# GpSimd's split of the value weights waits in addition for the scaled late values: an attention and mixture-of-experts block on one core

## The reference

```python
h = layernorm(x) * (1 + ca) + sa                      # x: 4 batches x 1024 tokens x 256
normed = h * rsqrt(mean(h * h) + EPS)
q, k, v = split(normed @ W_qkv.T + b_qkv)             # 16 heads of 64
scores = where(causal_mask, -inf, einsum('bqhd,bkhd->bhqk', q, k))
attn = softmax(scores, axis=-2)                       # over the QUERIES, for each key
x = x + ga * (einsum('bhqk,bkhd->bqhd', attn, v) @ W_o.T + b_o)
h = layernorm(x) * (1 + cb) + sb
x = x + gb * moe(h)                                   # 16 experts, top 1, 256 slots each
```

## Time and profile before

| what | value |
|---|---|
| median of 3 runs | 1401.01 us (1400.46 to 1401.9) |
| the profiled execution: its time, its span | 1402.89 us, 1401.1 us |
| busy: PE, PEld, DVE, ACT, POOL | 88%, 62%, 60%, 41%, 23% |
| mean granted TensorE clock | 0.941 of full speed; 0.89 from 60 to 351 us, 1.00 from 351 to 1036 us |
| attention steps with an odd `pp` | 16, with a split of the value weights at 92, 157, 222, 286, 351, 413, 475, 537, 599, 660, 722, 784, 846, 907, 968 and 1029 us |

### The profile page before, as it was taken

How to read it: one execution, slowest core, us unless ns; L and a number is a source line. 1 busy time by engine, 2 the same in 40 slices (tenths; PEclk the granted TensorE clock), 3 DMA queues, 4 the chain that set the end, 5 groups by cost and what they waited for, 6 DMA issues and landing times.

```text
span 1401.1 us, 24008 instructions
## 1 busy us (share of the span) xinstructions
PE 1235.5 (88%) x7256; PEld 867.0 (62%) x7256; DVE 839.9 (60%) x2166; ACT 574.4 (41%) x1387; POOL 325.7 (23%) x487
## 2 busy tenths in 40 slices
PE   2588888888999999999999999999988629999995
PEld 0455555555666666666666566666656518888884
DVE  4465656656766777677666666666665533444443
ACT  0354555555455555555555555455541001111110
POOL 2221111211232323222233312212221530111111
PEclk8788899999999999999999999999998859999998
DMA  5311111111222122221121121112155862565630
GB/s 194 127 65 58 65 57 64 57 45 43 69 65 71 64 66 83 67 68 64 63 71 64 64 80 60 55 58 74 60 188 201 290 216 101 176 239 180 227 109 18
DMA packets 99118, 139.55 MB, mean 100 GB/s; under 512 B 9848, under 2 KB 71162, under 8 KB 98808
## 3 DMA queue, kind: packets, MB, share of 16 engines
q1 hardware_dynamic: 90504, 113.81, 24.7%
q10 hardware_dynamic: 4464, 16.25, 2.8%
q0 software_dynamic: 4096, 8.82, 1.6%
HBM read 94.76 MB, written 48.00 MB: 102 GB/s over the span
## 4 chain that ended last, share of the span: by engine, by line
PE 77%; issue 8%; ACT 5%; DVE 4%; DMA 3%; SPq 2%; POOL 1%; DVEq 0%; ACTq 0%; POOLq 0%
PE SC L653 19%; PE Z L671 17%; PE Z L818 8%; PE SC L792 8%; PE XA L703 6%; PE XA L625 5%; ACT E L853 4%; PE XB L625 4%; PE XA L635 4%; PE XB L635 3%; PE XB L690 1%; DMA out<-th 1%; DMA xb<-xh_s 1%; DVE nm L1065 0%; SPq L443 0%
## 5 line engine op out<-in xcount | busy, mean ns | idle before, releaser
L853 ACT ACTIVATE E<-SC,nm 128x512 f32<-128x512 f32 (+7 forms) x512 | 375.5, 740 | 436.7 <-DVE nm L1065 436.7
L1065 DVE CUSTOM_DVE_ANT_0 SC<-SC,mask 128x512 f32<-128x512 f32 (+7 forms) x512 | 375.8, 786 | 226.4 <-PE SC L653 226.4
L653 PE MATMUL SC<-XQ,XK 64*128 64x512 f32 (+3 forms) x2304 | 271.3, 368 | 51.5 <-ACT E L853 50.1
L653 PEld LDWEIGHTS SC<-XQ,XK 64*128 64x128 f32 x2304 | 188.7, 192 | 151.2 <-issue 134.2
L671 PE MATMUL Z<-E,vs 128*64 128x512 f32 (+3 forms) x1536 | 271.8, 496 | 4.0 <-DVE vs L1043 4.0
L671 PEld LDWEIGHTS Z<-E,vs 128*64 128x64 f32 x1536 | 100.3, 138 | 141.8 <-issue 127.0
L818 PE MATMUL Z<-W,hh 128*128 128x256 f32 x512 | 114.9, 383 | 2.2 <-DVE yb L1311 2.2
L792 PE MATMUL SC<-bT,W 128*128 128x256 f32 x512 | 113.9, 381 | 0.0
L818 PEld LDWEIGHTS Z<-W,hh 128*128 128x128 f32 x512 | 97.3, 192 | 15.6 <-DVE yb L1311 2.6
L792 PEld LDWEIGHTS SC<-bT,W 128*128 128x128 f32 x512 | 98.0, 192 | 13.4
L853 ACT ACTIVATION_READ_ACCUMULATOR E<-SC,nm 128x1 f32 x512 | 101.3, 198 | 0.0
(11 more groups left out here) (193 smaller groups left out, 1753.7 us busy)
## 6 DMA issues: line engine op xcount, KB each, us to landing
W<-in_w SPq DMA_DIRECT2D x32, 1024.0 KB, 8.5
z_s<-zs ACTq DMA_DIRECT2D x31, 512.0 KB, 2.6
zt<-z_s SPq DMA_DIRECT2D x24, 512.0 KB, 3.7
W<-in_wqk SPq DMA_DIRECT2D x33, 257.0 KB, 2.7
slots_s<-zt SPq DMA_DIRECT2D x16, 520.0 KB, 4.0
xb<-slots_s SPq DMA_DIRECT2D x16, 520.0 KB, 3.7
xb<-xh_s SPq DMA_DIRECT2D x24, 256.0 KB, 5.4
Wv<-in_wv SPq DMA_DIRECT2D x17, 256.0 KB, 2.6
```

The source lines that it names most:

```text
L653: last = pe.matmul(SC[h][:, at:at + z - a], XK[rows, ap, kp, lo:lo + P], XQ[rows, ap, qp, a:z], start=(t == 0), stop=(t == 2))
L853: act.activation(E[:, h, EOFF[kb]:EOFF[kb + 1]], SC[h][:, at:at + S - lo], ACT.Exp, bias=nm[:, h, kb:kb + 1], scale=-1.0, accum_out=rs[:, ...
L1065: dve.tensor_tensor_reduce(SC[h][:, at:at + S - lo], SC[h][:, at:at + S - lo], mask[:, 0:S - lo], 1.0, BIG, ALU.add, ALU.min, nm[:, h, kb: ...
```

## The change

GpSimd waits, before it splits the value weights at the end of an odd step, in addition for the third (late) scaling of values of that step. The work itself stays as it is.

```diff
                         pool.wait_ge(auxa_full, st.of("auxa", piece_use(st, ("v", 2))[1]))
                         pool.wait_ge(auxb_full, st.of("auxb", piece_use(st, ("v", 3))[1]))
+
+                        pool.wait_ge(s["vscaled"], st.of("vscaled", LATE + 1))
                         split_values_weights(st.b * COUPLES + st.j + 2)
```

## The result

The changed kernel takes 1389.56 us in the median of 17 runs (1386.2 to 1392.84), beside 1401.69 us for the kernel before, also 17 runs (1391.65 to 1405.15). The ratio is 0.9924, 95% interval 0.9905 to 0.9943: 8 to 13.3 us faster, 10.7 in the middle. Forecast were 9.1 us, with a time of 1391.9 in a range of 1386 to 1396.5. The profiled execution has a span of 1389.7 us instead of 1401.1.

A forecast was written before the change was run, and what follows sets the result against it. TensorE carries 77% of the chain and waits where GpSimd's split stretches VectorE's late scaling. Gains of 3.2 + 0.9 + 0.35 + 4.7 = 9.1 us off 1401.0 gave 1391.9 us, range 1386 to 1396.5.

The forecast's parts named there:

- The stretched scaling: VectorE's late scaling in odd steps, lengthened beside GpSimd's split, returns from 1.73 to 0.69 us; hTl comes 1.04 us earlier.
- Where the split goes: On GpSimd, the cast starts 0.95 us after the scaling's start; the split ends 1.75 us later, stretching nothing there.
- rival 3: The moved split blocks VectorE's first reduction of the next step: 15 us slower, 1416 us; chance 0.05.
- What is late next: xln's load on SyncE, behind the split, comes 1.75 us later and caps the second reduction's gain at 0.56 instead of 1.04.
- Rival 1: xln's load does not bind, so the whole gain of 15.5 us arrives: 1385.5 us; chance 0.11 with its neighbourhood.
- 0.35 (351): Split at 351 us, whose xln load took 4.03 us: 0.35 us gained if it lands in 2.3 to 2.5.
- 3.2 (six): Six splits from 413 to 723 us with xln's load behind them: slack sum 13.66 less 6 x 1.75, 3.2 us gained.
- 1.03 (785): Split at 785 us, with no xln load behind it: the uncapped gain of 1.03 us.
- 3.64 (batch 3): Four splits of batch 3, without hTl or an xln load behind them: 0.91 us gained each.
- Batch 0: Four early splits with slower xln landings: gains of 0.11, 0.44, 0.06 and 0.28, together 0.9 us.
- Rival 2: xln's load costs more through a later split and slower landings: 4.5 us less gain, 1396.4 us; chance 0.12.
- rival 4: The scaling is long for another reason than the split, so no change: 1401 to 1402.5 us; chance 0.04.

The follow-up runs named there:

- e7: Kernel before, GpSimd's subtraction replaced by a plain copy of Wv; time not read, scaling 1.13 to 1.14 us in eight odd steps, 0.96 to 1.07 in five, 0.69 in three.
- e8: Kernel before, GpSimd's subtraction replaced by a memset of the same tile; time not read, scaling 0.69 us in all odd steps.
- e2: Changed kernel, with SyncE issuing xln's load ahead of the wait for the split and Wv's load; 1377.97 us beside 1397.73 for the kernel before.
- e4: Kernel before, with only the split's subtraction waiting for the late scaling and the cast left in place; 1376.8 us beside 1397.73 for the kernel before.
- e5: Kernel before, with only the subtraction waiting for the late scaling and xln's load issued ahead of Wv's; 1378.8 us beside 1398.04 for the kernel before.
- e6: Changed kernel with the subtraction done twice, so the split ends about 1.4 us later; 1407.73 us beside 1398.04 for the kernel before.
- e10: Kernel before, unedited, profiled a third time as a single run; 1401.21 us.
- e9: Kernel before, unedited, profiled a second time as a single run; 1396.61 us.
- e1: Changed kernel again, no edit; 1387.34 us beside 1397.73 for the kernel before.
- e11: Changed kernel, unedited, profiled a third time as a single run; 1386.84 us.

## Why the prediction was right

**The stretched scaling.** As forecast, 0.69 us in 16 of 16 odd steps, and 1.04 us earlier hTl. TensorE's wait for hTl fell to 0.33, forecast 0.32. Shown by the trace and by e7 and e8: it is a lock on reading, not the amount of work.

**Where the split goes.** The cast was forecast 0.95 us behind the scaling's start, and starts 0.95 behind it. Nothing it meets there is stretched: rival 3 is out.

**What is late next.** This was the step on which the size hung, and it held: VectorE waits for xln 31.5 to 32.1 us in 11 steps (forecast about 32; the 4.1 us in 6 cases that the prediction gives for before hold one of 1.25 us at 45.6, ahead of all these steps). In the shown step the statistics start 3.28 us after the split's end (3.26 before). Rival 1 (the whole gain) became the truth only in e2, e4 and e5, once the load's order or the split's end was put right, and e6 shows the slope of the same cap from the other side.

**The sum by stretches.** For "rest" the terms were 0.35 (351), 3.2 (six), 1.03 (785) and 3.64 (batch 3), 8.2 us together. Measured: 7.3 to 7.8 against the first profile of before and e10 (707.1, 707.0), and up to 9.1 against e9, 1.3 of it from e9's slow last step. One small term was off: from the statistics' start to the second reduction it takes 1.04 us (597.73 to 598.77), not 0.95. With 0.09 less each, the 0.39 to 0.60 per couple of batch 1 and 2 become 0.30 to 0.51, and the first profile gave 0.25 to 0.50. Batch 3 gave 0.85 to 0.94 (forecast 0.91), and the step behind 785 gave 1.06 (1.03). The case at 351 landed in 2.4 us this time, as I had taken it.

**What was not in the sum, and luck.** Batch 0. I had 0.9 us for it; the three profiles of the changed kernel have 252.8, 256.5 and 255.0 us, those of before 258.9, 252.9 and 258.9. Most of that spread is TensorE's granted clock, which I had read at 0.89 in one execution and taken for constant. Where the clock is alike, less than the 0.9 shows: three couples of e1 (90.5 to 284.5 us) ran at 0.89 to 0.90 as before and took 194.0 us, as before, where the sum had 0.6. The medians differ by 10.4 and 12.1 us and the ratio gives 10.7, so 1.3 to 3 us more than forecast, with the 9.1 inside the interval. But the two runs of e1 with a mean clock of 0.947 or over are only 7.4 us under the three such runs of before, about what "rest" gives. So as far as these few runs show, the mechanism gave some 7.5 us, less than its 9.1, and the clock about 3, for which the sum had nothing. That the total came out so near is partly luck.

The changed kernel's mean clock is between the others: 0.946 in the mean of its 23 runs, 0.944 in the 29 of before beside the experiments, 0.949 in the 14 of e2, e4 and e5. The runs of either of the first two spread over 0.006 and more, so how much of the 3 us the change itself brings stays open.

**Rival 2** (xln costs more) and **rival 4** (another cause of the long scaling) are out by the same rows.

## What to carry to other kernels

When two engines stretch each other's instruction, look at which of them the path waits for and let that one start first; but then follow everything that the displaced work releases, down to the DMA queue of a third engine, because its slack caps the gain. Here a load that stood behind an unrelated wait in an in-order queue took about a third of the gain (4.1 of 11.8 us in "rest"), and more with the clock of batch 0; issuing it first, or delaying only the one instruction that collides, brings it back (1.5% instead of 0.7%). And where the clock is not steady, compare kernels stretch by stretch, and runs of like mean clock.

## What the runs showed of the hardware

- A VectorE tensor_tensor with two SBUF inputs and a GpSimd instruction that reads SBUF exclude each other, whichever starts first: the scaling went from 0.69 to 1.73 us beside a subtraction of 1.28, to 1.14 beside a copy of 0.62, and a copy from 0.62 to 1.09 behind a scaling of 0.69. Beside a memset of 0.53 nothing happened.
- In the records the block is a little shorter than the instruction that causes it: the scaling ended 0.56 us after the subtraction and 0.54 after the copy of e7 (at 589), though it takes 0.69 alone. Whether the block or only the recorded end of GpSimd's instruction is off by that 0.13 to 0.15 no run shows.
- The 1024-wide reduction (PSUM and SBUF in) beside GpSimd's cast and subtraction took 1.23 and 1.27 us, and 1.22 and 1.26 before, without them.
- After a TensorE wait of 2.24 us (e6, at 425) the granted clock was at a mean of 0.75 of full speed in the next 6.8 us, so it spent part of them at the lower of its two levels (1.2 and 2.4 GHz); after one of 2.16 us (e6, at 553) it stayed at 1.00. After those of 0.5 to 0.8 us in the changed kernel the matmuls kept their 1.3 us.
- With a wait of 3.6 to 4.9 us in each step of batch 0 the same step ran at a mean clock of 0.89 or of 0.94, from one execution of the same kernel to the next (e9 beside e10, e1 beside e11); in e9 a step is 0.6 to 1.4 us shorter at the higher one.
- With waits of 3.6 to 3.9 us there, and nothing late, four profiles of four (e2, e4, e5, e8) had the same six of nine steps at 0.94 to 0.95.
